# A Perceiver block: keys' refinement and scores' scaling ahead of a batch's first subtraction, and GpSimd's sum ahead of the last batch's first maximum

## The chip, the cores and the metric

The kernel runs on one core of a Trainium2 chip. The metric is the device time of one execution in microseconds (us), lower is better. The profile comes from one further execution, with its own time and span.

## The reference

Three blocks follow each other on x of shape (8, 64, 512), each added to x: a cross-attention on a context of shape (8, 1601, 256), a causal self-attention of 16 heads, and a feed-forward layer with ternary weights. The change lies in the first. Cut to what matters:

```python
q = rmsnorm((layernorm(x) @ Wq).reshape(B, Sq, H, D), gq)      # B=8, Sq=64, H=16, D=128
k = rmsnorm((context @ Wk).reshape(B, Skv, H, D), gk)          # Skv=1601
v = (context @ Wv).reshape(B, Skv, H, D)
attn = softmax(einsum('bqhd,bkhd->bhqk', q, k) / sqrt(D))
x = x + einsum('bhqk,bkhd->bqhd', attn, v).reshape(B, Sq, H * D) @ Wo
```

The softmax runs over 1601 context rows for each of 16 heads times 64 queries, 1024 columns a batch.

## The kernel before

**Precision.** Matrix products are made of three: a value is split in a high part (a cast on ScalarE) and a low part (`low_part`, line 42, a subtraction on VectorE), and `products` (lines 36 to 38) multiplies high by high, high by low and low by high. A block of such products with two halves of the contraction is six matmuls.

**The cross-attention.** The key weights are folded into the queries ahead of the loop, so the scores of a context tile come straight from the context (`scores`, tiles `fq_hi`, `fq_lo` and `cT_hi`, `cT_lo`). The keys themselves are made as well (`key_bank`, four banks of 512 columns a tile, tiles `wk_hi`, `wk_lo`), but only for the sum of their squares: ScalarE squares them where they lie (`key_square`, lines 1857 and 1863), VectorE takes the mean (`key_mean`, lines 1178 and 1182), ScalarE makes a first guess of the inverse root (`key_guess`, lines 1871 and 1879), and VectorE refines it in three operations on 128 x 16 values (`key_refine`, lines 1192, 1194 and 1198). `scale_scores` (line 1221, one operation of 1024 columns from PSUM and `k_rstd`) then writes the scaled scores into a ring of 14 slots.

**Softmax with a lag.** A batch is 13 tiles, and the loop has one step a tile (N = 104 steps). The maximum over a batch's rows must be known before its first tile can be subtracted, so each tile's second half of the work lags 14 steps behind its scores. At step s the kernel scores tile s-1 and works on an older tile u:

- `subtract_max(u)` (line 1253) on VectorE: ring minus `col_max`
- `exponential(u)` (line 1883) on ScalarE
- `numerator_hi(u)` (line 1890) and, one step later, `numerator_lo(u)` on VectorE, which split the numerators into `p_hi` and `p_lo`
- `track_sum(u)` on VectorE (`run_sum`, line 1287), and `weighted_context(u)` on TensorE

In a batch's first step (t = 0) GpSimd spreads the maximum of the batch before over the partitions (line 2259, `col_max`), and then, from the third batch on, the sum of the batch before that (line 2266, `col_sum`). In the second step (t = 1), u is the first tile of a batch and needs the new `col_max`. ScalarE turns `col_sum` into its reciprocal there (`sum_log`, `sum_guess`, lines 1906 and 1910), VectorE refines it (`sum_refine`, lines 1297 and 1299), and one step later divides the finished context by it (`evacuate`, line 1320).

**Order of the work.** Each engine has its own written-out order, and semaphores bind them. In a second step ScalarE's queue is: `key_square(s, 0)`, `key_square(s, 1)`, the cast `cT_hi` (line 1760), `exponential(u)`, `sum_log`, `sum_guess`, `key_square(s, 2)` (the one of line 1857, into `sq`), `numerator_hi(u)`, `key_square(s, 3)`, `high_cn`. TensorE alternates two banks for the keys, so a bank of keys can be written only when the bank two before it has been squared:

```python
pe.wait_ge(*free[kb])
...
free[kb] = (k_squared, NG * key_of[s] + g + 1)
```

**The last batch** (tiles from `LAST` = 91) takes its maximum in two parts: the first over its first eight tiles (`PART` = 8), at step 99, the second after the loop. From step 94 on, older tiles go two to a step, so that the lag shrinks. At step 99 GpSimd spreads the first maximum and the sum of the batch before. At step 100 `subtract_max(91)` needs that maximum.

Of the kernel before, what the change touches and what calls it, by code (L numbers as in the profile page):

```python
# [13 lines left out]
P = 128  # L14
# [26 lines left out]
def low_part(dve, lo, src, hi):  # L41
    return dve.tensor_tensor(lo, src, hi.bitcast(F32), ALU.subtract)  # L42


def perceiver_block(nc, x, ctx, ctxT, rest, restT, wq, wk, wkT, wv, wo, gq, gk, w_attn, b_qk, b_v, w_proj, b_proj,
# [12 lines left out]
    TT = -(-TK // P)  # L58
# [11 lines left out]
    with ExitStack() as whole:  # L70
        def sem(name):
            return whole.enter_context(nc.semaphore(name))
# [3 lines left out]
        def bank(i, n=1):  # L76
            return ps[:, i * BANK:(i + n) * BANK]
# [37 lines left out]
        run_max = keys.take("run_max", [P, HQ])  # L115
# [26 lines left out]
        tiles = [(b, t, P) for b in range(B) for t in range(TT)]  # L142
# [8 lines left out]
        key_of = {s: i for i, s in enumerate(key_tiles)}  # L151
# [17 lines left out]
        PART = 8  # L169
        LAST = (B - 1) * TT  # L170
# [3 lines left out]
        steps = [list(range(d - k, d)) for d, k in zip(slots_done, per_step)]  # L174
# [39 lines left out]
        col_max = work.take("col_max", [P, HQ])  # L214
        run_sum = work.take("run_sum", [P, HQ])
        sum_at = work.at
        col_sum = work.take("col_sum", [P, HQ])
# [139 lines left out]
        def row_count(r, step):  # L357
# [31 lines left out]
        scores_mm, scaled, maxed, max_spread = sem("scores_mm"), sem("scaled"), sem("maxed"), sem("max_spread")  # L389
        shifted, exped, p_hi_done, p_lo_done = sem("shifted"), sem("exped"), sem("p_hi_done"), sem("p_lo_done")  # L390
        summed, sum_spread, sum_guessed, sum_refined = (
            sem("summed"), sem("sum_spread"), sem("sum_guessed"), sem("sum_refined"))
# [45 lines left out]
        def max_count(s):  # L438

            return tiles[s][0] * (TT - 1) + max(tiles[s][1], 1)  # L440
# [3 lines left out]
        def refinements(s):  # L444

            return sum(4 if k in rest_tile[2:] else 3 for k in key_tiles if k <= s)
# [588 lines left out]
        def dve_program(dve):  # L1035
# [75 lines left out]
            for n in range(NQT + 3):  # L1111
# [4 lines left out]
                if n >= 3:  # L1116
                    i = n - 3
# [42 lines left out]
            def ring_slot(s):  # L1160
                return ring[0:tiles[s][2], s % RING]
# [48 lines left out]
            def scale_scores(s):  # L1210
                b, t, n = tiles[s]
                dve.wait_ge(scores_mm, s + 1)
                dve.wait_ge(k_refined, refinements(s))
                if s >= RING:
                    dve.wait_ge(p_lo_done, s - RING + 1)
                    dve.wait_ge(summed, sum_count(s - RING))
                dst = ring_slot(s).rearrange("p (h q) -> p h q", h=H)
                raw = bank(S_BANK, 2).rearrange("p (h q) -> p h q", h=H)
                if s not in rest_tile:
                    rstd = k_rstd[:, key_of[s] % 2].unsqueeze(2).broadcast_to([P, H, TQ])  # L1220
                    dve.tensor_tensor(dst, raw, rstd, ALU.mult).then_inc(scaled, 1)  # L1221
                else:
                    if b == 0:
                        dve.wait_ge(consts, 8)
                    rstd = left_rstd[:, b % 2].unsqueeze(2).broadcast_to([P, H, TQ])
                    dve.scalar_tensor_tensor(out=dst, in0=raw, scalar=left_mask[:, b % 2, b // 2:b // 2 + 1], in1=rstd,
                                             op0=ALU.add, op1=ALU.mult).then_inc(scaled, 1)
# [43 lines left out]
            def numerator_lo(u):  # L1271
                dve.wait_ge(p_hi_done, u + 1)
                hi, lo = numerators(u)
                low_part(dve, lo, ring_slot(u), hi).then_inc(p_lo_done, 1)
# [114 lines left out]
            for s in range(N):  # L1389
                slots = steps[s]  # L1390
                first, last = slots[:1], slots[-1:]
                if s == 0:
                    for c in range(KC):
                        fold_copy(NG - 1, c)
                if s == 0:
                    dve.wait_ge(ln_norm, MT)
                    dve.memset(row_scales[:], 0.0).then_inc(row_steps, 1)
                if s == 1:
                    for k in range(KC):
                        low_fq(0, k)  # L1400
                    dve.wait_ge(fold_kept, KC * NG)
                    for c in range(KC):
                        dve.wait_ge(fold_out[c], 16 * NG)
                    dve.tensor_scalar(ones[:], ident[:], 0.0, 1.0, ALU.mult, ALU.add).then_inc(ones_done, 1)

                for u in first:
                    new_max = tiles[u][1] == 0 or u == HELD - 1
                    if not new_max:
                        for v in SUB_IN.get(u, [u]):
                            subtract_max(v)  # L1410
                    if u > 0:
                        numerator_lo(u - 1)
                    if new_max:
                        for v in SUB_IN.get(u, [u]):
                            subtract_max(v)
                    if u > 1 and tiles[u - 1][1] == 0:
                        evacuate(tiles[u - 1][0] - 1)
                for u in slots[1:]:
                    subtract_max(u)
                if s - 1 in key_of:  # L1420
                    key_refine(s - 1)
                for u in first:
                    track_sum(u)
                    if u == HELD - 1:
                        track_sum(HELD)
                for u in slots[1:]:
                    low_cn(u - 1)
                    numerator_lo(u - 1)
                if s > 0:
                    scale_scores(s - 1)  # L1430
                    track_max(s - 1)
                for e in [e for e in range(len(cT_seq)) if cT_step[e] == s and tiles[s][1] > 0]:
                    low_cT(e)
                for u in slots[1:]:
                    track_sum(u)
                if s in row_at:
                    row_groups(row_at[s])
                if tiles[s][0] + 1 < B and tiles[s][1] in FQ_STEPS:
                    low_fq(tiles[s][0] + 1, FQ_STEPS.index(tiles[s][1]))
                if s in piece_at:  # L1440
                    ternary_round(piece_at[s])
                for e in [e for e in range(len(cT_seq)) if cT_step[e] == s and tiles[s][1] == 0]:
                    low_cT(e)
                for u in slots:
                    if u > 0 and tiles[u - 1][1] == TT - 1:
                        sum_refine(tiles[u - 1][0])
                if s == N - 1:
                    numerator_lo(HELD - 1)
                    numerator_lo(HELD)
                if s in key_of:  # L1450
                    key_mean(s)
                for u in last if s < N - 2 else (HELD - 2, HELD - 1) if s == N - 2 else (HELD, HELD + 1):
                    low_cn(u)
                if s in EARLY_CN:
                    low_cn(EARLY_CN[s])
# [237 lines left out]
            for f in range(FT):  # L1693
                i = f % 2
# [515 lines left out]
        def pool_program(pool):  # L2210
# [36 lines left out]
            for parity, rows in enumerate(halves):  # L2247
                single = halves[1 - parity]
                pool.memset(left_mask[rows, parity], 0.0).then_inc(consts, 1)
                pool.tensor_scalar(left_mask[single, parity], ident[single, single.start:single.start + B // 2], LEFT_OUT,  # L2250
                                   -LEFT_OUT, ALU.mult, ALU.add).then_inc(consts, 1)
            for s in range(N):
                i = s - 1
                if i >= 0 and (tiles[i][1] == TT - 1 or i == LAST + PART - 1):
                    b = tiles[i][0]
                    pool.wait_ge(maxed, max_count(i))
                    if b > 0:
                        pool.wait_ge(shifted, b * TT)
                    pool.partition_all_reduce(col_max[:], run_max[:], P, bass.bass_isa.ReduceOp.max).then_inc(max_spread, 1)  # L2259
                for u in steps[s]:  # L2260
                    if u < LAST and tiles[u][1] == TT - 1:
                        b = tiles[u][0]
                        pool.wait_ge(summed, (TT - 1) * (b + 1))
                        if b > 0:
                            pool.wait_ge(sum_refined, 2 * b)
                        pool.partition_all_reduce(col_sum[:], run_sum[:], P,
                                                  bass.bass_isa.ReduceOp.add).then_inc(sum_spread, 1)


            pool.wait_ge(maxed, max_count(N - 1))  # L2270
# [346 lines left out]
```

## Time and profile before

| what | value |
|---|---|
| time, median of 3 runs | 1456.44 us (1455.81 to 1457.22) |
| the profiled execution's own time | 1456.01 us |
| its span in the profile | 1454.2 us |
| TensorE busy | 1433.1 us, 99% of the span |
| VectorE busy | 1241.1 us, 85% |
| ScalarE busy | 996.7 us, 69% |
| GpSimd busy | 165.2 us, 11% |
| TensorE's mean granted clock | 0.998 of full speed |

The span is what the profile shows of the 1456.01 us; 1.8 us lie around it. Engine names in the rows are PE (TensorE matmuls), PEld (its weight loads), DVE (VectorE), ACT (ScalarE), POOL (GpSimd). A busy share is an average over stages with different limits, so the stage around the change has to be read by itself.

### The profile page before, as it was taken

How to read it: one execution, taken by the hardware profiler on the slowest of the kernel's cores; microseconds unless marked ns; L12 is line 12 of the kernel's file. 1: busy time of each engine (PE TensorE's matmuls, PEld its weight loads, DVE VectorE, ACT ScalarE, POOL GpSimd, SP SyncE). 2: the span in 40 equal slices, each digit the busy share in tenths (PEclk: the TensorE clock that was granted, in tenths of full speed). 3: DMA queues.
4: the chain of work that ended last, by engine and by line, in shares of the span. 5: the costliest groups of instructions: out<-in, count | busy, mean ns of one | idle time of the engine just before them, and what ended most of it. 6: DMA issues, size and time to landing. Idle time of an engine off the chain costs nothing.

```text
span 1454.2 us, 22226 instructions
## 1 busy us (share of the span) xinstructions
PE 1433.1 (99%) x6829; PEld 1178.2 (81%) x6829; DVE 1241.1 (85%) x1996; ACT 996.7 (69%) x3689; POOL 165.2 (11%) x119
## 2 busy tenths in 40 slices
PE   8999999999999999999999999999999989999998
PEld 7778888888888888888888888888888777887887
DVE  8746889999999999999999998988898899777543
ACT  5676777776777777677777767777767567647432
POOL 2210000002000200110010002000200210124342
PEclk9999999999999999999999999999999999999999
DMA  6542332222222132223322331221221143641000
GB/s 203 177 135 84 106 88 75 82 80 71 82 87 81 62 104 91 64 67 89 89 73 69 103 91 44 84 59 59 62 66 37 44 139 111 218 174 60 1 0 29
DMA packets 105621, 125.15 MB, mean 86 GB/s; under 512 B 10912, under 2 KB 80288, under 8 KB 104352
## 3 DMA queue, kind: packets, MB, share of 16 engines
q1 hardware_dynamic: 98208, 116.40, 25.9%
q10 hardware_dynamic: 7296, 7.34, 1.5%
q8 instruction: 55, 0.90, 0.3%
q14 instruction: 62, 0.51, 0.1%
HBM read 101.59 MB, written 22.12 MB: 85 GB/s over the span
## 4 chain that ended last, share of the span: by engine, by line
PE 81%; DVE 12%; issue 3%; ACT 2%; DMA 0%; POOL 0%; DVEq 0%; ACTq 0%; POOLq 0%; SPq 0%
PE ps L36 25%; PE ps L38 25%; PE ps L37 25%; DVE ring L1253 3%; DVE p_lo L42 2%; PE ps L990 2%; PE ps L991 2%; PE ps L1008 1%; PE ps L1009 1%; DVE ring L1221 1%; ACT ps L1863 1%; PE ps L863 1%; DVE wq_lo L42 0%; DVE k_sum L1178 0%; DMA wq_raw<-in_wq 0%
## 5 line engine op out<-in xcount | busy, mean ns | idle before, releaser
L1863 ACT ACTIVATE ps<-ps 128x128 f32<-128x128 f32 x1212 | 316.3, 261 | 119.7 <-PE ps L38 118.1
L36 PE MATMUL ps<-wk_hi,cT_hi 128*128 128x512 f32 x808 | 315.7, 391 | 1.2 <-ACT sq L1857 0.5
L38 PE MATMUL ps<-wk_hi,cT_lo 128*128 128x512 f32 x808 | 314.4, 389 | 0.0
L37 PE MATMUL ps<-wk_lo,cT_hi 128*128 128x512 f32 x808 | 314.4, 389 | 0.0
L1863 ACT ACTIVATION_READ_ACCUMULATOR ps<-ps 128x1 f32 x1212 | 224.1, 185 | 0.0
L36 PEld LDWEIGHTS ps<-wk_hi,cT_hi 128*128 128x128 f32 x808 | 151.7, 188 | 36.6 <-issue 3.4
L38 PEld LDWEIGHTS ps<-wk_hi,cT_lo 128*128 128x128 f32 x808 | 151.7, 188 | 31.6
L37 PEld LDWEIGHTS ps<-wk_lo,cT_hi 128*128 128x128 f32 x808 | 151.7, 188 | 31.0
L36 PE MATMUL ps<-fq_hi,cT_hi 128*128 128x512 f32 x416 | 161.9, 389 | 0.9 <-DVE ring L1221 0.9
L38 PE MATMUL ps<-fq_hi,cT_lo 128*128 128x512 f32 x416 | 161.8, 389 | 0.0
L37 PE MATMUL ps<-fq_lo,cT_hi 128*128 128x512 f32 x416 | 161.8, 389 | 0.0
L36 PE MATMUL ps<-p_hi,cn_hi 128*128 128x512 f32 x400 | 155.8, 390 | 3.6 <-DVE p_lo L42 2.0
L38 PE MATMUL ps<-p_hi,cn_lo 128*128 128x512 f32 x400 | 155.6, 389 | 0.0
L37 PE MATMUL ps<-p_lo,cn_hi 128*128 128x512 f32 x400 | 155.6, 389 | 0.0
L1253 DVE TENSOR_TENSOR ring<-ring,col_max 128x1024 f32<-128x1024 f32 x99 | 143.7, 1454 | 1.4 <-POOL col_max L2259 1.4
L1221 DVE TENSOR_TENSOR ring<-ps,k_rstd 128x1024 f32<-128x1024 f32 x96 | 117.2, 1221 | 27.6 <-PE ps L38 25.0
L1883 ACT ACTIVATE ring<-ring 128x1024 f32<-128x1024 f32 x104 | 109.3, 1051 | 43.1 <-DVE ring L1253 42.8
L2259 POOL PARTITION_ALL_REDUCE col_max<-run_max x8 | 26.6, 3321 | 979.7 <-DVE run_max L1244 979.7
L42 DVE TENSOR_TENSOR p_lo<-ring,p_hi 128x1024 fp32r<-128x1024 f32 x104 | 135.4, 1303 | 0.0
L1890 ACT CAST p_hi<-ring 128x1024 fp32r<-128x1024 f32 x104 | 108.4, 1042 | 7.0 <-PE ps L38 7.0
L1244 DVE TENSOR_TENSOR run_max<-run_max,ring 128x1024 f32<-128x1024 f32 x88 | 107.8, 1225 | 3.0
L1287 DVE TENSOR_TENSOR run_sum<-run_sum,ring 128x1024 f32<-128x1024 f32 x83 | 101.3, 1220 | 2.9 <-ACT ring L1883 2.4
(244 smaller groups left out, 2656.7 us busy)
## 6 DMA issues: line engine op xcount, KB each, us to landing
cT_raw<-in_ctxT SPq DMA_DIRECT2D x96, 128.0 KB, 2.8
cn_raw<-in_ctx SPq DMA_DIRECT2D x96, 128.0 KB, 2.3
row_raw<-in_wgu SPq DMA_DIRECT2D x32, 256.0 KB, 2.8
w_raw<-in_wguT SPq DMA_DIRECT2D x32, 256.0 KB, 2.6
qk_scratch<-folded ACTq DMA_DIRECT2D x8, 896.0 KB, 4.2
fq_raw<-qk_scratch SPq DMA_DIRECT2D x14, 512.0 KB, 3.9
pc_scratch<-pc_out SPq DMA_DIRECT2D x7, 1024.0 KB, 4.2
pc_raw<-pc_scratch SPq DMA_DIRECT2D x8, 896.0 KB, 8.1
```

Source lines behind the costliest of these rows:

```text
L36: pe.matmul(dst, l_hi, r_hi, start=first, stop=False)
L37: pe.matmul(dst, l_hi, r_lo, start=False, stop=False)
L38: return pe.matmul(dst, l_lo, r_hi, start=False, stop=last)
L42: return dve.tensor_tensor(lo, src, hi.bitcast(F32), ALU.subtract)
L990: pe.matmul(bank(bk)[:, toks], wt[:, blk, k, ws], zT_hi[:, k, toks], start=k == 0, stop=False)
L1221: dve.tensor_tensor(dst, raw, rstd, ALU.mult).then_inc(scaled, 1)
L1244: dve.tensor_tensor(run_max[0:n], run_max[0:n], ring_slot(s), ALU.max).then_inc(maxed, 1)
L1253: dve.tensor_tensor(ring_slot(u), ring_slot(u), top_of[0:n], ALU.subtract).then_inc(shifted, 1)
L1287: dve.tensor_tensor(run_sum[0:n], run_sum[0:n], ring_slot(u), ALU.add).then_inc(summed, 1)
L1863: done = act.activation(head, head, ACT.Square, accum_out=k_sum[:, i, g * GH + h:g * GH + h + 1])
L1883: act.activation(ring_slot(u), ring_slot(u), ACT.Exp).then_inc(exped, 1)
L1890: act.copy(numerators(u)[0], ring_slot(u)).then_inc(p_hi_done, 1)
```

## The change

In a second step, between `numerator_lo(u - 1)` and `subtract_max(u)`, VectorE now does `key_refine(s - 1)` and `scale_scores(s - 1)`, which before came behind the subtraction. This holds for the seven steps in which u is the first tile of one of the first seven batches (steps 14, 27, 40, 53, 66, 79 and 92); the last batch's (step 100) keeps its order. On GpSimd, at step 99 alone, the sum of the seventh batch goes ahead of the last batch's first maximum. No operation is added or taken away, and no DMA is touched.

```diff
                     if u > 0:
                         numerator_lo(u - 1)
+                    if tiles[u][1] == 0 and u < LAST:
+
+                        key_refine(s - 1)
+                        scale_scores(s - 1)
                     if new_max:
                         for v in SUB_IN.get(u, [u]):
                             subtract_max(v)
...
-                if s - 1 in key_of:
+                scores_first = bool(first) and tiles[first[0]][1] == 0 and first[0] < LAST
+                if s - 1 in key_of and not scores_first:
                     key_refine(s - 1)
...
+                if s > 0 and not scores_first:
+                    scale_scores(s - 1)
                 if s > 0:
-                    scale_scores(s - 1)
                     track_max(s - 1)
...
+            def spread_max(i):
+                b = tiles[i][0]
+                pool.wait_ge(maxed, max_count(i))
+                if b > 0:
+                    pool.wait_ge(shifted, b * TT)
+                pool.partition_all_reduce(col_max[:], run_max[:], P, bass.bass_isa.ReduceOp.max).then_inc(max_spread, 1)
+
+            def spread_sum(b):
+                pool.wait_ge(summed, (TT - 1) * (b + 1))
+                if b > 0:
+                    pool.wait_ge(sum_refined, 2 * b)
+                pool.partition_all_reduce(col_sum[:], run_sum[:], P, bass.bass_isa.ReduceOp.add).then_inc(sum_spread, 1)
+
             for s in range(N):
...
+                sums = [tiles[u][0] for u in steps[s] if u < LAST and tiles[u][1] == TT - 1]
+                if s - 1 == LAST + PART - 1:
+
+                    for b in sums:
+                        spread_sum(b)
+                    spread_max(s - 1)
+                else:
+                    if s > 0 and tiles[s - 1][1] == TT - 1:
+                        spread_max(s - 1)
+                    for b in sums:
+                        spread_sum(b)
```

## Rows read from the trace of the kernel before

**Rows 1.** Busy microseconds of each engine in two stretches, TensorE's granted clock, DMA.

```profile
350.00:477.00 127.00, 127.00 (x562) 105.21 (x561) 119.55 (x201) 96.37 (x393) 0.00 (x0) 1.00 0.29 87
...
1150.00:1188.00 38.00, 33.50 (x146) 26.81 (x145) 37.02 (x50) 24.24 (x84) 0.00 (x0) 1.00 0.17 54
```

**Rows 2.** Timeline of GpSimd: start, duration, work, idle time before it.

```profile
335.31 3.32 POOL L2259 PARTITION_ALL_REDUCE col_max<-run_max  x1 [131.51 <-DVE run_max L1244]
338.53 6.96 POOL L2266 PARTITION_ALL_REDUCE col_sum<-run_sum  x1
...
1139.20 6.21 POOL L2266 PARTITION_ALL_REDUCE col_sum<-run_sum  x1
```

**Rows 3.** Timeline of VectorE in the third batch's second step.

```profile
337.73 0.92 DVE L1182 TENSOR_SCALAR k_mean<-k_sum 128x16 f32<-128x16 f32 x1 [1.59 <-ACT ps L1863]
...
338.30 1.22 DVE L42 TENSOR_TENSOR p_lo<-ring,p_hi 128x1024 fp32r<-128x1024 f32 x1
339.43 5.56 DVE L1253 TENSOR_TENSOR ring<-ring,col_max 128x1024 f32<-128x1024 f32 x1
344.91 0.16 DVE L1192 TENSOR_TENSOR k_step<-k_rstd 128x16 f32<-128x16 f32 x1
...
345.59 1.23 DVE L1221 TENSOR_TENSOR ring<-ps,k_rstd 128x1024 f32<-128x1024 f32 x1
346.73 0.42 DVE L42 TENSOR_TENSOR cT_lo<-cT_raw,cT_hi 128x256 fp32r<-128x256 f32 x1
```

**Rows 4.** That subtraction over the whole kernel: count, shortest, median, longest in ns.

```profile
L1253 DVE TENSOR_TENSOR ring<-ring,col_max x99: 1209/1218/5557, 203.8 to 1189.0; 128x1024 f32<-128x1024 f32 x99
```

**Rows 5.** Timeline of ScalarE, in the third batch's second step.

```profile
345.02 1.06 ACT L1883 ACTIVATE ring<-ring 128x1024 f32<-128x1024 f32 x1 [1.66 <-DVE ring L1253]
345.99 1.04 ACT L1906 ACTIVATE recip<-col_sum 128x1024 f32<-128x1024 f32 x1
...
348.03 0.58 ACT L1857 ACTIVATE sq<-ps 128x512 f32<-128x512 f32 x1
```

**Rows 6.** Timeline of TensorE in the same stretch, and one row at 769 us.

```profile
342.79 0.39 PE L38 MATMUL ps<-fq_hi,cT_lo 128*128 128x512 f32 x1
...
348.23 0.39 PE L38 MATMUL ps<-p_hi,cn_lo 128*128 128x512 f32 x1
348.75 0.47 PE L36 MATMUL ps<-wk_hi,cT_hi 128*128 128x512 f32 x1
...
769.60 0.47 PE L36 MATMUL ps<-wk_hi,cT_hi 128*128 128x512 f32 x1 [0.36 <-ACT sq L1857]
```

**Rows 7.** Timeline of all engines in the second batch's second step.

```profile
201.32 1.15 DVE L1182 TENSOR_SCALAR k_mean<-k_sum 128x16 f32<-128x16 f32 x1
...
203.83 1.22 DVE L1253 TENSOR_TENSOR ring<-ring,col_max 128x1024 f32<-128x1024 f32 x1 [1.35 <-POOL col_max L2259]
...
204.07 0.39 PE L38 MATMUL ps<-fq_hi,cT_lo 128*128 128x512 f32 x1
...
206.06 0.58 ACT L1857 ACTIVATE sq<-ps 128x512 f32<-128x512 f32 x1
...
207.01 0.39 PE L36 MATMUL ps<-wk_hi,cT_hi 128*128 128x512 f32 x1
```

**Rows 8.** Timeline of VectorE, then of ScalarE, where the last batch's maximum begins.

```profile
1131.50 1.23 DVE L1287 TENSOR_TENSOR run_sum<-run_sum,ring 128x1024 f32<-128x1024 f32 x1 [0.17 <-ACT ring L1883]
...
1138.79 0.53 DVE L1182 TENSOR_SCALAR k_mean<-k_sum 128x16 f32<-128x16 f32 x1 [1.98 <-ACT ps L1863]
...
1139.35 5.56 DVE L42 TENSOR_TENSOR p_lo<-ring,p_hi 128x1024 fp32r<-128x1024 f32 x1
...
1149.38 1.22 DVE L1297 TENSOR_TENSOR pc_out<-col_sum,recip 128x1024 f32<-128x1024 f32 x1
...
1144.03 0.39 ACT L1760 CAST cT_hi<-cT_raw 128x256 fp32r<-128x256 f32 x1
```

**Rows 9.** Timeline of TensorE behind it.

```profile
1156.67 0.47 PE L36 MATMUL ps<-p_hi,cn_hi 128*128 128x512 f32 x1 [1.56 <-DVE pc_out L1320]
```

More of the change, by code:

```diff
@@ L2251, in pool_program @@
                                    -LEFT_OUT, ALU.mult, ALU.add).then_inc(consts, 1)
-            for s in range(N):
[L2253 to L2267, printed above, removed]
+            def spread_max(i):
[9 more added lines that the diff above has]
+                pool.partition_all_reduce(col_sum[:], run_sum[:], P, bass.bass_isa.ReduceOp.add).then_inc(sum_spread, 1)
+            for s in range(N):
+                sums = [tiles[u][0] for u in steps[s] if u < LAST and tiles[u][1] == TT - 1]
[8 more added lines that the diff above has]
+                        spread_sum(b)
             pool.wait_ge(maxed, max_count(N - 1))
```

## The prediction, made before the changed kernel ran

> **What bounds the kernel now.** I read the busy time by stretch first. In the loop of the cross-attention TensorE is busy for every microsecond between two batch boundaries (127.00 of 127.00 at full clock) while VectorE has 119.55; only behind 1150 us, in the last batch, does TensorE idle (33.50 of 38) and VectorE take over (37.02 of 38) [rows 1]. So an edit in the loop costs or gives what it adds to or takes from TensorE's waits, and in the last batch what it does to VectorE's chain. The next views are the timelines of the engines around one batch boundary.
>
> GpSimd's maximum ends at 338.63 and its sum starts at 338.53 [rows 2]. VectorE is then in `p_lo`, which ends at 339.52. The subtraction that follows, normally 1.22 us, takes 5.56 us and ends at 344.99 [rows 3]; over the kernel its median is 1218 ns and its longest 5557 [rows 4]. Five of the six boundaries that have a sum look like this one; in the sixth (1038 us) and at 1139 us the same 5.6 us fall on `p_lo` [rows 8]. I read it as GpSimd taking something that VectorE needs, at the first gap between two of VectorE's instructions, and holding it: 344.99 minus 1.22 is 343.77, 4.25 us after `p_lo` ended.
>
> What hangs on that subtraction is ScalarE: its exponential starts at 345.02, right behind, and from it logarithm, exponential and the squares of a keys' bank follow without a gap, the squares at 348.03 [rows 5]. TensorE, whose pace is one matmul each 0.226 us (562 in 127 us) [rows 1], puts its next one at 348.75 in place of 348.46, and at 769.60 the trace names the squares as what ended the same wait [rows 6]. So each boundary has one tight chain: GpSimd's sum, VectorE's subtraction, ScalarE's four operations, TensorE's next bank of keys. There is no slack in it, and 0.3 us of it are already paid.
>
> **The change, part by part.** Six of the seven moved pairs (steps 27 to 92) lie in such a boundary. The moved work is three small refinements and one scaling. From the start of the first refinement at 344.91 to the start of the scaling at 345.59 are 0.68 us, and from there to the next instruction's start at 346.73 are 1.14 us [rows 3]. Together 1.82 us go in front of the subtraction. Does the wait hide them? The refinement is now the instruction behind `p_lo`. It reads two tiles in the on-chip memory, as the blocked subtraction and the blocked `p_lo` do, and size is no protection: `k_mean`, 128 x 16 like the `k_step` of 0.16 us, took 0.92 us under the maximum [rows 3]. I take the refinement as blocked until 343.77. Then the scaling starts at 344.45, the subtraction at 345.59, and it ends at 346.81 in place of 344.99. The three refinements hold VectorE's queue, so the scaling is no help in the blocked time.
>
> Other bound: the refinement slips through. Then the scaling still waits for the scores, whose last matmul starts at 342.79 and ends at 343.18 [rows 6]; it runs from 343.22, the subtraction from 344.36 to 345.58: 0.59 us late. So the cost of one such boundary lies between 0.59 and 1.82 us, and nothing in it can be below zero, because those scores are late by themselves. I take 1.82, since the same kind of instruction is seen blocked. ScalarE's chain moves by as much (the sum it also needs is ready at 345.49, before the old 345.99), and so does TensorE, which was waiting for it already: 6 x 1.82 = 10.92 us. What the early scaling could give, an earlier free PSUM bank, nobody waits for: TensorE's next scores come behind the keys' bank. The low part of the context's tile (346.73) stays where it is, since only the order ahead of it changes. `sum_refine` waits for ScalarE and moves with it.
>
> A rule speaks on this too: the Trainium skill, SBUF — State Buffer, section "Who interferes with whom", says that a VectorE instruction with two inputs in SBUF contends with a GpSimd instruction that reads SBUF, and that one with a single SBUF input doesn't. By that rule the scaling (PSUM and `k_rstd`) would run during the sum, and only the refinements ahead of it would block; that gives the same sum. The rows so far agree for two inputs.
>
> The seventh pair, step 14, has a maximum but no sum. The old subtraction began at 203.83, behind the maximum. The scaling now ahead of it needs scores whose last matmul ends at 204.07 + 0.39 = 204.46, so it starts at 204.50, and the subtraction at 205.64 instead: 1.81 us late. The squares move from 206.06 to 207.87 and end at 208.45; TensorE wanted their bank at 207.01 and gets it at about 208.59 (0.14 us behind the end, as at 348.61 to 348.75) [rows 5 to 7]. Cost 1.58 us; bounds 1.4 and 1.8.
>
> The swap at step 99: `track_sum` ends at 1132.73, so the sum can start at 1132.82 rather than 1139.20, and takes 6.2 us, to 1139.0 [rows 2, 8]. It holds VectorE until about 1137.3 (1139.20 to 1143.69 was 4.5 us after its start, with `p_lo` in it). GpSimd's old maximum began 3.3 us before 1139.20, at 1135.9, right behind VectorE's running maximum; held until 1137.3, that one (1.2 us) now ends near 1138.5, which is 2.6 us late, and 1.98 us of that fall into VectorE's idle time ahead of `k_mean` [rows 8]. The maximum on GpSimd starts at 1139.0 and ends at 1142.3. `k_mean` may be held by its first part: the one at 201.32 was released at 202.30, 1.5 us before the maximum's end at 203.8 [rows 7], which here is 1140.8. Then come `cn_lo`, `p_lo`, and the subtraction at 1142.4, where it began at 1144.8 behind the held `p_lo`: 2.4 us earlier. But the exponential behind it on ScalarE can't go before the cast at 1144.03 [rows 8], so it starts at about 1144.34, and 3.1 us later the reciprocal is there, at 1147.45. `sum_refine`, which started at 1149.38, starts 1.9 us earlier, and VectorE's chain behind it with it. TensorE waits for that chain: 1.56 us at 1156.67 for the evacuation [rows 9] and again at the following scores. From there VectorE sets the pace [rows 1], so I carry the 1.9 to the end. Bounds: 0 (the held VectorE and the ordering behind two reductions eat it) and 2.4 (VectorE's own lead). If the scaling at step 99 were blocked too, the maximum would come at 1139.8 and the subtraction at 1143.2, still not later than the cast allows.
>
> Sum: 10.92 + 1.58 - 1.91 = +10.6 us on the profiled execution's 1456.01, so 1466.6; its span of 1454.2 becomes 1464.8. The median of the three runs lies 0.43 higher, which gives 1467.0.
>
> **The rivals.**
>
> Slip-through. The tiny refinements get past GpSimd (they run from 339.5, before its hold takes effect). Five boundaries cost 0.59, the sixth, where `p_lo` itself is held and the refinement comes behind the hold in any case, 1.82. For it: GpSimd has to win at the gap behind `p_lo`, and the trace shows this only against a large instruction there. Against: GpSimd has then been asking for 1.0 us (338.53 to 339.52), and at 1139.35 and 1038 us it won within 0.2 us. Sum: 2.95 + 1.82 + 1.58 - 1.91 = +4.4, 1460.9 as a median.
>
> No gain at the end. Boundaries as forecast, but the two reductions in a row at step 99 cost VectorE what they give. Sum: +12.5, 1468.9. Against: the 1.98 us of VectorE's idle time absorb most of the hold [rows 8].
>
> The other side: TensorE catches up. If the 0.227 us pace of its matmuls were set by something with spare speed behind a stall, the 12.5 us at the boundaries would be won back within a batch's 130 us, and only the 1.91 us gained at the end would stay: 1454.5, 0.13% faster. It decides from a pace of 0.223 us or less (3 ns saved on each of 562 matmuls are 1.8 us). Against: the stretch from 350 us lies right behind the wait at 348.75, TensorE is busy in all of it, and it still holds only 562 matmuls, 0.226 us each [rows 1, 6]; the lost 0.3 us isn't made up there.
>
> **How the numbers follow.** Forecast 0.78 with its end effects from 0 to 2.4 us: 1466.5 to 1468.9 by its terms, 1465.5 to 1469.5 with the run-to-run spread. Slip-through 0.11. No gain at the end 0.05. Catching up 0.04, something unseen 0.02. The range runs from 1460.0 (slip-through with the larger end gain) to 1470.0. A measurement of this kernel tells a change from none at about 0.2%, 2.9 us: 1453.5 to 1459.4 is no change. Slip-through at +4.4 counts as slower mostly. That gives slower 0.91, same 0.07, faster 0.02.
>
> **What the changed profile would show.** In each of the six second steps the long instruction is no longer the subtraction but the first `k_step` (about 4.4 us in place of 0.16), except in the sixth, where it stays `p_lo`; the subtraction is back at 1.22 everywhere; TensorE's gap ahead of `wk_hi,cT_hi` has grown from 0.3 to 2.1 us; a new one of 1.6 us stands near 207 us; the waits at 1156 and 1160 us (old time) are gone or smaller, and the sum at step 99 starts ahead of the maximum, with `run_max` as the long one. The prediction is wrong if `k_step` stays at 0.2 us, if ScalarE has room between exponential and squares, or if TensorE's matmuls come closer than 0.227 us behind a gap.

## The result, and the profile after

The changed kernel takes 1469.65 us (median of 5 runs, 1466.60 to 1470.22) against 1456.04 us (5 runs): a ratio of 1.0085, 95% interval 1.0073 to 1.0096, slower by 12.4 us (10.6 to 14.0) by that ratio, which is taken over all runs; the two medians lie 13.6 us apart. The forecast was 1467.0 with a range of 1460 to 1470. The profiled execution took 1466.60 us with a span of 1464.8, which are the 1466.6 and 1464.8 of the forecast's sum. The four other runs took 1469.2 to 1470.2 at a mean granted clock of 0.996 to 0.997 in place of 0.998. So there are two things to read: the 10.6 us of the profile, and the 3 us that most runs have on top. One later execution of the changed kernel ran with TensorE's clock at about half throughout (0.556 of full speed, 2406.64 us) and is left out of every comparison.

**The stretches.** Busy time in the columns of [rows 1], behind a boundary that was full before, in ten microseconds around a boundary, and at the end:

```profile
350.00:477.00 127.00, 125.05 (x553) 103.58 (x553) 118.24 (x198) 97.14 (x394) 0.00 (x0) 1.00 0.28 84
490.00:500.00 10.00, 8.05 (x36) 6.39 (x35) 7.07 (x10) 7.40 (x25) 0.55 (x1) 1.00 0.02 4
1150.00:1188.00 38.00, 35.16 (x154) 28.46 (x154) 36.47 (x49) 26.14 (x97) 4.47 (x2) 1.00 0.13 46
```

TensorE's 127 us hold 553 matmuls in place of 562, and ten microseconds around a boundary only 36. The clock is at full speed. The end has gained: 35.16 of 38 us busy in place of 33.50 (the work there is not the same to the microsecond).

**The third batch's second step on VectorE**, against [rows 3]:

```profile
339.69 1.22 DVE L42 TENSOR_TENSOR p_lo<-ring,p_hi 128x1024 fp32r<-128x1024 f32 x1
340.83 4.51 DVE L1192 TENSOR_TENSOR k_step<-k_rstd 128x16 f32<-128x16 f32 x1
...
345.85 1.23 DVE L1221 TENSOR_TENSOR ring<-ps,k_rstd 128x1024 f32<-128x1024 f32 x1
346.99 1.22 DVE L1253 TENSOR_TENSOR ring<-ring,col_max 128x1024 f32<-128x1024 f32 x1
...
351.36 1.23 DVE L1297 TENSOR_TENSOR pc_out<-col_sum,recip 128x1024 f32<-128x1024 f32 x1 [2.83 <-ACT recip L1916]
```

The long instruction is now the first `k_step`: 128 x 16 values, 4.51 us in place of 0.16. It starts where `p_lo` ends, and is held for 4.3 us. The scaling and the subtraction (1.22 us again) come behind it, and `sum_refine` then waits 2.83 us for ScalarE. At the boundaries every subtraction is back at 1.2 us. (One of 2.92 us at 1199.36 lies under GpSimd's second maximum, behind the loop.) TensorE's waits in this step and, as the sixth of them, at 1061 us, against [rows 6]:

```profile
351.96 0.47 PE L36 MATMUL ps<-wk_hi,cT_hi 128*128 128x512 f32 x1 [1.95 <-ACT sq L1863]
...
1061.08 0.47 PE L36 MATMUL ps<-wk_hi,cT_hi 128*128 128x512 f32 x1 [1.99 <-ACT sq L1863]
```

The wait is now long enough that the trace names its cause: ScalarE's squares. The step from 348.23 to 348.75 has become a gap of 1.95 us. Over the six boundaries it is 1.95 to 1.99 us at five and 2.16 at the fourth, which had 0.36 before.

**Step 14**, without a sum, against [rows 7]:

```profile
202.75 0.18 DVE L1192 TENSOR_TENSOR k_step<-k_rstd 128x16 f32<-128x16 f32 x1 [0.53 <-ACT k_rstd L1885]
...
204.24 1.23 DVE L1221 TENSOR_TENSOR ring<-ps,k_rstd 128x1024 f32<-128x1024 f32 x1 [0.90 <-PE ps L38]
205.39 1.22 DVE L1253 TENSOR_TENSOR ring<-ring,col_max 128x1024 f32<-128x1024 f32 x1
...
208.32 0.47 PE L36 MATMUL ps<-wk_hi,cT_hi 128*128 128x512 f32 x1 [1.40 <-ACT sq L1863]
```

The refinement runs free (0.18 us), the scaling waits 0.90 us for its scores, and TensorE then waits 1.40 us.

**Step 99.** GpSimd's two reductions, then VectorE and ScalarE, against [rows 8]:

```profile
1145.15 6.11 POOL L2269 PARTITION_ALL_REDUCE col_sum<-run_sum  x1 [90.29 <-DVE run_sum L1287]
1151.17 3.30 POOL L2263 PARTITION_ALL_REDUCE col_max<-run_max  x1
```

```profile
1145.72 1.22 DVE L1221 TENSOR_TENSOR ring<-ps,k_rstd 128x1024 f32<-128x1024 f32 x1 [0.66 <-PE ps L38]
1146.97 3.79 DVE L1244 TENSOR_TENSOR run_max<-run_max,ring 128x1024 f32<-128x1024 f32 x1
...
1151.73 1.44 DVE L1182 TENSOR_SCALAR k_mean<-k_sum 128x16 f32<-128x16 f32 x1
...
1154.55 1.21 DVE L1253 TENSOR_TENSOR ring<-ring,col_max 128x1024 f32<-128x1024 f32 x1
...
1159.78 1.23 DVE L1297 TENSOR_TENSOR pc_out<-col_sum,recip 128x1024 f32<-128x1024 f32 x1 [0.36 <-ACT recip L1916]
```

```profile
1156.35 0.39 ACT L1766 CAST cT_hi<-cT_raw 128x256 fp32r<-128x256 f32 x1
1156.65 1.06 ACT L1889 ACTIVATE ring<-ring 128x1024 f32<-128x1024 f32 x1
```

GpSimd's sum starts while VectorE is idle, in the 0.66 us ahead of the scaling. The scaling starts 0.57 us into the sum and takes its usual 1.22 us; the running maximum behind it, with two inputs on chip, takes 3.79; the subtraction follows the new maximum at once; and the exponential starts at the cast's end, not at the subtraction's start. TensorE's wait for the evacuation is gone, and the next one is smaller, against [rows 9]:

```profile
1170.98 0.47 PE L36 MATMUL ps<-fq_hi,cT_hi 128*128 128x512 f32 x1 [0.82 <-DVE ring L1221]
```

**Where the time came from.** GpSimd's maxima mark the boundaries, so their starts in both traces give the shift from one to the next. The changed trace is 0.26 us ahead at the first of them, before any edit takes effect (200.23 against 200.49). From there the shift grows by 1.65 us for step 14, then by 1.84, 1.84, 1.80, 1.80 and 1.81 for five boundaries. The sixth can't be told from the swap this way; at the last batch's second maximum, behind both, the change stands at 10.39 us (1188.01 to 1198.40), or 10.65 with the 0.26 of the start, and the spans differ by 10.6. So the sum of the prediction holds term by term in this execution, in which the granted clock is full everywhere in the loop. (It is 0.83 at 1230 to 1240 us, where the shift hardly moves.)

### The profile page after: what moved, and what is told of

Its sections match the earlier page's. It is cut to its first block, busy times and chain, and to the rows that moved or that the text cites. A ratio compares the mean times of both kernels' runs of the same rounds, so it can differ in the third digit from the quotient of the medians.

```text
span 1464.8 us, 22226 instructions
## 1 busy us (share of the span) xinstructions
PE 1433.6 (98%) x6829; PEld 1179.2 (81%) x6829; DVE 1240.7 (85%) x1996; ACT 996.8 (68%) x3689; POOL 165.1 (11%) x119
## 4 chain that ended last, share of the span: by engine, by line
PE 81%; DVE 11%; issue 4%; ACT 3%; DMA 0%; POOL 0%; SPq 0%; DVEq 0%; ACTq 0%; POOLq 0%
PE ps L36 25%; PE ps L38 25%; PE ps L37 25%; DVE p_lo L42 2%; PE ps L990 2%; PE ps L991 2%; DVE ring L1253 2%; DVE k_step L1192 2%; ACT ps L1869 1%; PE ps L1008 1%; DVE ring L1221 1%; PE ps L1009 1%; PE ps L863 1%; ACT recip L1912 0%; DMA wq_raw<-in_wq 0%
## 5 line engine op out<-in xcount | busy, mean ns | idle before, releaser
L42 DVE TENSOR_TENSOR p_lo<-ring,p_hi 128x1024 fp32r<-128x1024 f32 x104 | 131.1, 1261 | 0.0
L1253 DVE TENSOR_TENSOR ring<-ring,col_max 128x1024 f32<-128x1024 f32 x99 | 122.1, 1236 | 0.0
```

The lines of the kernel that those rows point to most:

```text
L1253: dve.tensor_tensor(ring_slot(u), ring_slot(u), top_of[0:n], ALU.subtract).then_inc(shifted, 1)
```

## The experiments

All are built on the kernel before or the changed one, and compared with runs of the kernel before on the same chip. Differences in us are between medians.

**The batches' part alone.** The new order on VectorE, GpSimd as before (the changed kernel without the second part of its diff).

> VectorE's new order at the seven second steps, GpSimd's order of before. Theory (the refinement stands still behind GpSimd's sum, then refinement and scaling go ahead of the subtraction): six boundaries at 1.82 us and one at 1.58 us, nothing given back at the end, so +12.5 us against the kernel before (span about 1466.7). Rival (most of the loss comes from the two reductions in a row at step 99): this one would stay near +1 to +3 us.

Measured 1473.98 us against 1457.02: 1.0112 (1.0098 to 1.0126), +16.3 us, and its profile +20.0. From maximum to maximum the shift grows by 1.69, 3.44, 1.83, 3.39, 2.54, 3.41 and 1.82 us. Step 14 and two boundaries cost what the theory says; four cost more: 1.6 us three times and 0.7 once, 5.5 us together. Those are the places where the granted clock is low. Columns as in [rows 1]:

```profile
340.00:350.00 10.00, 10.00 (x46) 8.26 (x44) 8.72 (x9) 4.56 (x21) 7.23 (x2) 1.00 0.09 26
350.00:360.00 10.00, 8.05 (x29) 6.22 (x28) 8.19 (x10) 8.52 (x33) 0.00 (x0) 0.83 0.05 13
490.00:500.00 10.00, 8.05 (x36) 6.39 (x35) 6.95 (x9) 6.28 (x16) 2.48 (x1) 1.00 0.00 0
1180.00:1190.00 10.00, 7.99 (x28) 6.15 (x27) 9.22 (x10) 5.97 (x15) 0.00 (x0) 0.83 0.05 13
```

350 to 360 us and 490 to 500 us are the same place of two batches, with the same 8.05 us of busy time. At full clock there are 36 matmuls in it, at 0.83 there are 29: seven less, at 0.227 us each 1.6 us. The last row is a fifth such fall, in the last batch, and costs 1.6 us too (19.73 us of shift at the second maximum, 18.16 at the first). TensorE's rows behind the gap show the fall begin and end:

```profile
352.30 0.47 PE L36 MATMUL ps<-wk_hi,cT_hi 128*128 128x512 f32 x1 [1.95 <-ACT sq L1863]
...
352.84 0.42 PE L38 MATMUL ps<-wk_hi,cT_lo 128*128 128x512 f32 x1
...
353.91 0.63 PE L38 MATMUL ps<-wk_hi,cT_lo 128*128 128x512 f32 x1
...
356.47 0.41 PE L38 MATMUL ps<-fq_hi,cT_lo 128*128 128x512 f32 x1
...
357.41 0.39 PE L36 MATMUL ps<-wk_hi,cT_hi 128*128 128x512 f32 x1
```

The third matmul behind the gap starts 0.23 us after the second (0.42 us long), from 353.5 on they start 0.43 us apart (0.63 each), and from 356.7 on 0.23 again: 3.4 us at half clock (1.2 in place of 2.4 GHz). TensorE had been without a gap for over 130 us before; what stands ahead of the fall is the 1.95 us wait. The same gap at 497.56 us has no fall behind it, nor has the sixth, at 1066.94, and in the trace of the changed kernel none of six like gaps has one. So the loss has a part that is there whatever the clock does, 12.6 us, and a part that comes and goes. The rival, loss at step 99, falls.

**The swap at step 99 alone.** VectorE as before.

> VectorE's order of before, only GpSimd's swap at step 99. Theory: the last batch's first subtraction comes 2.4 us earlier, ScalarE's cast limits that to 1.9 us, VectorE's chain carries it to the end: -1.9 us. Rival (the hold on the running maximum eats it): 0.

Measured 1454.74 against 1457.02: 0.9984 (0.9975 to 0.9993), -2.3 us. The swap is a gain by itself. Its profile ended where that of before did, with a granted clock of 0.83 at 1160 to 1170 us, behind a wait of the last batch that the kernel before has as well. Columns as in [rows 1], then the matmul ahead of the fall:

```profile
1160.00:1170.00 10.00, 7.98 (x28) 6.08 (x27) 9.51 (x11) 5.72 (x13) 0.00 (x0) 0.83 0.05 13
...
1165.41 0.51 PE L36 MATMUL ps<-p_hi,cn_hi 128*128 128x512 f32 x1 [2.02 <-DVE p_lo L42]
```

From GpSimd's maximum at step 99 to the last batch's second one, this trace takes 48.82 us; the changed kernel's, with the same order there and no fall, takes 47.23 (1151.17 to 1198.40). So the fall costs 1.6 us, which is what hides the swap's gain in this profile. Falls are thus not tied to the new gaps: the kernel before scatters too, 21 runs of it from 1455.6 to 1458.5 us at mean clocks of 0.997 to 1.0.

**The refinement alone ahead.**

```diff
                     if tiles[u][1] == 0 and u < LAST:
                         key_refine(s - 1)
-                        scale_scores(s - 1)
...
-                if s > 0 and not scores_first:
+                if s > 0:
                     scale_scores(s - 1)
```

> GpSimd's order of before; at the seven second steps only the three small refinements go ahead of the subtraction, the scaling stays behind it. Theory: the first refinement takes the hold of 4.3 us, and only 0.68 us (its start to the scaling's start) go ahead of the subtraction in six boundaries; at step 14 the refinement ends before the maximum does and costs nothing: +4.1 us. Rival (the cost comes from the hold itself becoming longer when a small instruction meets it): near +12. Rival (small instructions slip through): 0, and the subtraction keeps its 5.56 us.

Measured 1.0022 (1.0012 to 1.0031), +2.6 us at the median, +3.3 in the profile, where the forecast had +4.1; 0.48 to 0.54 us a boundary, step 14 nothing. VectorE's refinement and, behind it, TensorE's wait:

```profile
339.44 4.51 DVE L1192 TENSOR_TENSOR k_step<-k_rstd 128x16 f32<-128x16 f32 x1
...
349.27 0.47 PE L36 MATMUL ps<-wk_hi,cT_hi 128*128 128x512 f32 x1 [0.64 <-ACT sq L1862]
```

The hold is on `k_step`, and only the refinement's own length passes on, 0.5 us rather than 0.68. Neither the slip-through (the subtraction is short here) nor a longer hold holds up. The remaining 1.3 us of a boundary are the scaling's, by difference.

**ScalarE's squares first**, on the batches' part alone.

```diff
+                squares_first = bool(slots) and tiles[slots[0]][1] == 0 and slots[0] < LAST
+                if squares_first:
+                    key_square(s, 2)
                 for u in slots[:1]:
                     if tiles[u][1] == 0:
                         exponential(u)
...
-                key_square(s, 2)
+                if not squares_first:
+                    key_square(s, 2)
```

> As the first of these four, and ScalarE makes the third bank's squares ahead of the exponential in the seven steps, so that TensorE's next bank of keys no longer waits for the subtraction. If the keys' bank were the only way in which the lateness reaches TensorE, the loss would be gone (-2 to 0 us). Theory: VectorE's chain (sum refinement, then evacuation) is still 1.8 us late, and TensorE waits for the evacuation in its next step, about 1.6 us in six boundaries; at step 14 nothing: about +10 us, with the waits now named after the evacuation.

Measured 1.0078 (1.0064 to 1.0092), +11.6 us. In its profile the shift grows from 0.50 us at the first maximum to 11.66 at the last batch's, so 11.2 us: 0.58 for step 14 and 1.72 to 1.83 for each of the six others. (The clock recorded for this execution is 0.95 throughout, but 46 matmuls in ten microseconds are the pace of full clock.) TensorE now has two named gaps in place of one:

```profile
353.14 0.50 PE L36 MATMUL ps<-wk_hi,cT_hi 128*128 128x512 f32 x1 [0.73 <-ACT ps L1869]
...
358.35 0.47 PE L36 MATMUL ps<-p_hi,cn_hi 128*128 128x512 f32 x1 [0.53 <-DVE pc_out L1320]
```

The keys' bank that it waited for is free; the bank after next is not (ScalarE's four heads, line 1869), and then the evacuation. VectorE's chain is late as a whole, and the lateness comes out by another door. A third wait between the two, 0.15 us ahead of 356.15, is too short to be named. The forecast +10 had 1.6 us for each of six boundaries, by the evacuation alone, and nothing for step 14; it was short by 1.2 us in the profile and by 1.6 at the median. Against the batches' part alone the timed median is 5.4 us lower (1468.63 against 1473.98). Of that, 1.4 are less lateness (11.2 against 12.6, most of it at step 14); the rest, 4 us, is the size of two to three falls, and the trace has none in the loop.

**Without the sum, old order and new order.** A fill of `col_sum` with a constant, which only writes, in place of the sum; the kernels leave out the division by the true sums in seven batches.

```diff
-                        pool.partition_all_reduce(col_sum[:], run_sum[:], P,
-                                                  bass.bass_isa.ReduceOp.add).then_inc(sum_spread, 1)
+                        pool.memset(col_sum[:], 1600.0).then_inc(sum_spread, 1)
```

> The kernel before with GpSimd's sum over the partitions left out: a fill of col_sum with a constant stands in its place, which only writes. Theory (the sum's reads hold VectorE): no VectorE instruction of over 2 us is left at the boundaries, the subtraction is 1.22 us, TensorE's 0.3 us at six boundaries go, and the last batch's subtraction moves up until ScalarE's cast limits it: -1.8 - 1.9 = -3.7 us. Rival (VectorE is held by the maximum, which stays): the long instruction stays and so does the time.

> VectorE's new order, GpSimd's order of before, and the sum left out as in the run beside it. This prices the slip-through bound: the refinement runs free, but the scaling ahead of the subtraction still has to wait for its scores, so the subtraction ends 0.59 us later than in the kernel before. Theory: 6 x 0.59 + 1.58 - 1.9 = +3.2 us against the kernel before, +6.9 against the old order without the sum. Rival (without the hold the order doesn't matter): both without the sum are equal, -3.7 us.

Measured 0.9957 (0.9943 to 0.9971), -5.5 us, and 1.0025 (1.0015 to 1.0035), +4.1 us (+2.9 in the profile): 9.6 us apart, 9.3 in the profiles. The old order gains 1.8 us more than forecast: from maximum to maximum the six boundaries give 0.39 to 0.43 us four times, but 0.93 and 1.49 in two, where the forecast had 0.3 each; why those two give more stays open. The new order was forecast at +3.2. No instruction of 4 us is left at the boundaries of either. The fill isn't without effect: it lasts 1.03 us, and `k_mean` beside it and the maximum takes 1.83. But the subtraction behind it takes 1.22, and the scaling then waits for its scores in any case. The new order's step, VectorE and then TensorE:

```profile
341.61 0.17 DVE L1192 TENSOR_TENSOR k_step<-k_rstd 128x16 f32<-128x16 f32 x1 [0.53 <-ACT k_rstd L1885]
...
344.75 1.23 DVE L1221 TENSOR_TENSOR ring<-ps,k_rstd 128x1024 f32<-128x1024 f32 x1 [2.54 <-PE ps L38]
345.89 1.22 DVE L1253 TENSOR_TENSOR ring<-ring,col_max 128x1024 f32<-128x1024 f32 x1
...
350.87 0.47 PE L36 MATMUL ps<-wk_hi,cT_hi 128*128 128x512 f32 x1 [0.72 <-ACT sq L1863]
```

The refinement is free, but the scaling waits 2.54 us for its scores with the subtraction behind it, and TensorE still loses 0.6 us a boundary against the kernel before (0.56 to 0.62 in five of them from maximum to maximum, 0.41 in one). The old order puts the subtraction in that idle time: without the sum its subtraction starts at 338.92 and its scaling at 342.70, behind a wait of 2.06 us. So the new order costs without any hold too: the rival, that the order doesn't matter then, falls.

**The sum first at every boundary, old order and new order.**

```diff
             for s in range(N):
+                for b in [tiles[u][0] for u in steps[s] if u < LAST and tiles[u][1] == TT - 1]:
+                    spread_sum(b)
+                if s > 0 and (tiles[s - 1][1] == TT - 1 or s - 1 == LAST + PART - 1):
+                    spread_max(s - 1)
```

> VectorE's order of before, and GpSimd's sum ahead of the maximum at every boundary, not only at step 99. Theory: the sum's hold moves to the running maximum, ahead of the time where VectorE waits for ScalarE anyway; the subtraction comes up to 1.3 us earlier, ScalarE is no longer late for the keys' bank: 6 x -0.3 and -1.9 at the end, -3.7 us. Rival (the maximum comes later because the sum is ahead of it): the subtraction is later by some tenths and the time goes up by 1 to 6 us.

> The changed kernel with GpSimd's sum first at every boundary. Theory: no hold falls on the refinement any more, but the scaling's wait for its scores puts the subtraction 0.6 us behind that of before: 6 x 0.6 + 1.58 - 1.9 = +3.3 us. If the new order were good in itself and only met the sum at the wrong place, this one would be the fastest of all, below -3.7.

Measured for the old order: 1451.93 us against 1456.34, 0.9966 (0.9953 to 0.9978), -4.4 us (forecast -3.7), faster than both kernels. For the new order: 1461.36, 1.0028 (1.0018 to 1.0038), +5.0 (+4.4 in the profile, forecast +3.3). In the old order, GpSimd, VectorE and ScalarE:

```profile
333.21 6.12 POOL L2263 PARTITION_ALL_REDUCE col_sum<-run_sum  x1 [129.09 <-DVE run_sum L1287]
339.24 3.30 POOL L2257 PARTITION_ALL_REDUCE col_max<-run_max  x1
...
334.34 4.49 DVE L1244 TENSOR_TENSOR run_max<-run_max,ring 128x1024 f32<-128x1024 f32 x1
...
342.62 1.21 DVE L1253 TENSOR_TENSOR ring<-ring,col_max 128x1024 f32<-128x1024 f32 x1
...
343.90 0.39 ACT L1760 CAST cT_hi<-cT_raw 128x256 fp32r<-128x256 f32 x1
344.19 1.06 ACT L1883 ACTIVATE ring<-ring 128x1024 f32<-128x1024 f32 x1
```

The hold falls on the running maximum (4.49 us), and part of it on time in which VectorE waited for ScalarE before (1.59 us ahead of `k_mean` in [rows 3], nothing here). Counted from the maximum at 200 us, GpSimd's maximum starts 3.6 us later than in the kernel before, and yet the subtraction ends 1.5 us earlier (at 343.83 against 344.99, and this trace is already 0.33 us late at 200 us). It comes at once behind the maximum, because nothing of GpSimd's lies between the two any more. The exponential starts behind ScalarE's cast. In the loop TensorE is full again:

```profile
350.00:477.00 127.00, 127.00 (x562) 105.18 (x561) 118.98 (x200) 95.76 (x388) 1.72 (x1) 1.00 0.29 87
1150.00:1188.00 38.00, 35.18 (x154) 28.50 (x153) 37.13 (x47) 22.94 (x73) 4.13 (x1) 1.00 0.27 90
```

In the new order the scaling's wait for its scores (0.37 us) and its own 1.14 us stand ahead of the subtraction once more, and the boundaries cost again:

```profile
345.22 1.23 DVE L1221 TENSOR_TENSOR ring<-ps,k_rstd 128x1024 f32<-128x1024 f32 x1 [0.37 <-PE ps L38]
346.36 1.22 DVE L1253 TENSOR_TENSOR ring<-ring,col_max 128x1024 f32<-128x1024 f32 x1
```

**The changed kernel again.**

> The changed kernel once more, unchanged, for the size that the forecast missed. Its one profile had a span of 10.6 us over that of before, as forecast, but its other runs were 3 us longer at a lower mean granted clock. Theory: TensorE's granted clock falls behind some of the new 2 us gaps, for about 3.4 us and not in each run; each fall costs 1.6 us (as four did in the run with the batches' part alone). So runs between 1466.6 and about 1472 us, and a profile whose falls stand right behind gaps of TensorE. Rival (the 3 us come from elsewhere, a transfer or GpSimd): the lower clock stands where TensorE is not waiting.

The execution that was profiled is the one of 2406.64 us, so no trace shows where the clock fell in a slower run of the changed kernel: the expectation's theory and its rival, on the place of the falls, both stay untested. The four other runs: 1467.27 at a mean clock of 0.998, 1469.83 and 1470.59 at 0.996, 1472.47 at 0.994. Together with the five of the result the time follows the clock: 1466.6 and 1467.3 at 0.998, 1469.2 at 0.997, 1469.7 to 1470.6 at 0.996, 1472.5 at 0.994, or about 1.5 us for each 0.001 (5.9 us over 0.004). A fall of 3.4 us at half clock is 0.0012 of a run's mean and cost 1.6 us, so 1.4 us for each 0.001. The slower runs thus fit two to four falls more than the fastest; the means don't tell where.

**The changed kernel with ScalarE's squares first**, the edit shown above.

> The changed kernel with ScalarE's squares of the third bank ahead of the exponential in the seven steps. This splits each new gap of TensorE of 1.95 us into ones of 0.73 and 0.53 us and leaves the lateness (11.65 us in the run with the batches' part alone) where it is. Theory of the clock: without the long gaps there are no falls at the boundaries, so the median falls to about 11.65 - 2.1 = +9.6 us, near 1466, and its runs lie closer together than those of the changed kernel. Rival (the clock falls whatever the gaps are): median as the changed kernel's, 1469 to 1470.

Measured 1466.75 against 1457.03: 1.0067 (1.0054 to 1.0081), +9.7 us, five runs from 1465.4 to 1467.2. Its profile (+9.5 us) has no fall anywhere in the loop, and the mean clocks are 0.997 to 1.0. Against 1470.59 for the changed kernel beside it, 3.8 us are back. Not all of that is the clock's: the boundaries cost nearly the same (1.71 to 1.87 us), but step 14 costs 0.61 in place of 1.65, and from the first maximum to the last the shift is 9.26 us in place of 10.65. So 1.4 us are less lateness, and about 2.4 are left for the clock.

**The sum first and the squares first.**

> VectorE's order of before, GpSimd's sum first at every boundary (the fastest so far, -4.4 us), and ScalarE's squares first in the seven steps as well. TensorE has no gap left at the boundaries there, so there is nothing for the squares to give: the same as without them within 1 us, 1452. If it were faster by more, the keys' bank would still have been a wait.

Measured 1456.07 against 1457.03, 0.9991 (0.9982 to 1.0): a gain of 1.0 us in place of 4.4 without the squares first. The forecast missed. The squares now stand ahead of an exponential that was not late any more, and ScalarE waits 0.65 us for TensorE to finish the keys that it is to square. The exponential starts 6.20 us after GpSimd's maximum in place of 4.95 (344.89 and 338.69 against 344.19 and 339.24). In the next step TensorE starts the matmuls that need the evacuated banks late. The row of their weight load shows a wait and names no releaser, so that it is the evacuation's lateness is read from its place alone:

```profile
355.28 0.19 PEld L36 LDWEIGHTS ps<-p_hi,cn_hi 128*128 128x128 f32 x1 [0.46 <-issue]
```

From the first maximum to the one at step 99 this costs 3.2 us against the run without it. The profile has a fall of the clock at 1160 to 1170 us as well (0.83), worth 1.6 us by the stretch behind step 99 (48.80 against 47.23 us), and one at 1220 to 1230, worth 0.4 us at most.

## Why the prediction was right, point by point

- **TensorE is the bound in the loop, so a boundary's lateness goes to the end**: shown. From the first maximum to the last the shift is 10.65 us, and the spans differ by 10.6.
- **The refinement is held behind GpSimd's sum, then 1.82 us go ahead of the subtraction**: shown, in the changed trace (`k_step` 4.51 us, five boundaries at 1.80 to 1.84 us), and by the run with the refinement alone. The sixth boundary, with the hold on `p_lo` (5.60 us in the trace of after, too), cost 1.82 in the run with the batches' part alone. The working from 344.91 to 346.73 was exact for the sum; its split was not: the refinement is worth 0.5, the scaling 1.3.
- **The slip-through bound of 0.59 us**: it did not occur, but its price is right; without the sum the boundaries cost about 0.6 against the kernel before.
- **The chain over ScalarE's squares**: right as the door that is tightest, and TensorE's wait now carries their name. It isn't the only one: with the squares moved, the lateness of the six boundaries came out almost whole (1.72 to 1.83 us) at the next bank and at the evacuation; that of step 14 shrank to 0.58.
- **Step 14**: 1.65 us measured in the shift of the changed kernel, 1.69 in the batches' part alone; 1.58 forecast. TensorE's new gap is 1.40 us where 1.6 was forecast.
- **Step 99, -1.91**: the shift went from 10.48 us at the seventh maximum to 10.39 behind the sixth boundary and the swap; with 1.82 for that boundary the swap gave 1.91. ScalarE's cast was the limit, as worked out. The swap alone measured -2.3 at the median.
- **The rule of the Trainium skill** (SBUF — State Buffer, "Who interferes with whom") agrees with two more rows: at step 99 the scaling, with one input in SBUF and one in PSUM, ran its usual 1.22 us while the sum was holding, and the running maximum behind it, with two in SBUF, was held. The page says that one SBUF input is free of contention only outside VectorE's two-port modes, which the prediction leaves out; `k_mean`, with one input in SBUF, took 1.44 us under the maximum there and takes 0.17 where GpSimd is idle, and no run here tests whether that is this exception.
- **Catching up**: no sign of it; 553 matmuls in the 125.05 busy us of the stretch with the gap are 0.226 us each, as before. (The prediction's 3 ns on each of 562 matmuls are 1.7 us and not 1.8; nothing hangs on it.)
- **What the sum lacked**: the clock. It took the lengthened gap at its own length. The median is 2.65 us above the 1467.0, and inside the range only since that was drawn wide for other reasons; that part of the hit is luck. That a fall can stand behind a 2 us gap is seen in one trace, of the batches' part alone: behind four of its six. For the changed kernel it isn't shown. It rests on the clock means of its runs and on the 2.4 us or so that came back with the gaps split, beyond the lesser lateness. The rival, that the slower runs have their falls in the last batch, is open: falls at 1160 us and later stand in the profiles of the changed kernel and of at least five experiments, four of which have no 2 us gap in the loop; the kernel before has waits of 1.72 and 2.04 us there already. Against it: of the ten traces without a 2 us gap in the loop none has a fall in the loop. Why one gap has a fall behind it and the next equal one has not stays open.

## What to carry to other kernels

Before moving work in front of a waiting instruction, ask whether the moved work can itself run in that wait: here its first piece needs what GpSimd holds, and its second piece needs scores that come no sooner, so all of it went on top of the wait. Look instead at what makes the wait and whether that can be done when nobody needs the resource; GpSimd's sum, started ahead of its maximum at every boundary, gave 4.4 us with VectorE's order untouched. And on a TensorE that is busy without a break, allow for a new gap of about 2 us costing more than its length in some executions: here up to 1.6 us more, behind four gaps of twelve in two traces.

## What the runs showed of the hardware

Gaps of 1.95 to 2.16 us in a TensorE that is otherwise full were followed in four of six boundaries of one execution by some 3.4 us at half clock, worth 0.7 to 1.6 us each, and in none of six of another execution; gaps of 0.73 and 0.53 us in the same places by none in two profiles with them. An instruction of 128 x 16 values is held as long by GpSimd's sum as one of 128 x 1024: 4.3 us. The maximum's start being late is not the subtraction being late: with the sum first the maximum began 3.6 us later and the subtraction was ready 1.5 us sooner.
